# A state-space kernel in which 38 sums of GpSimd become accumulating transfers

## The reference, cut to what matters

```
def step(h, inputs):
    d_t, x_t, B_t, C_t = inputs
    dA = jnp.exp(d_t[..., None] * A)
    h = dA * h + (d_t * x_t)[..., None] * B_t[:, None, :]
    y = jnp.einsum('bds,bs->bd', h, C_t)
    return (h, y)
...
_, ys = jax.lax.scan(step, h0, xs)
y = ys.transpose(1, 0, 2) + xi * D
y = y * jax.nn.silu(z)
return x + y @ out_proj
```

## Time and profile before

| | |
|---|---|
| median of 3 runs | 586.09 us (582.63 to 587.27) |
| the profiled execution | 584.61 us, its span 582.8 us |
| mean granted TensorE clock | 0.935 |
| busy: PE, DVE, POOL, ACT | 81%, 79%, 69%, 64% of the span |

### The profile page before, as it was taken

One profiled execution on the slowest core, in us unless ns is written; L12 is line 12 of the kernel. 1 busy time (PEld: TensorE's weight loads), 2 busy tenths in 40 slices (PEclk: granted clock), 3 DMA queues, 4 the chain that ended last, 5 costly groups with the idle time before them and its releaser, 6 DMA issues.

```text
span 582.8 us, 7918 instructions
## 1 busy us (share of the span) xinstructions
PE 473.5 (81%) x2753; PEld 336.4 (58%) x2753; DVE 461.4 (79%) x531; ACT 374.3 (64%) x650; POOL 404.1 (69%) x253
## 2 busy tenths in 40 slices
PE   8968988778668899988678899795798758889992
PEld 6424655455547565745466466564686546678651
DVE  4779969988996678979987679789989989961512
ACT  3766667679764666788757567897747758821210
POOL 5049799859895599879883998888869979610001
PEclk9979999978998999869999999699999989999997
DMA  9331011111011011110210101101101292029004
GB/s 287 103 111 36 37 37 37 38 38 36 37 36 37 0 38 58 51 40 1 70 40 1 36 37 39 37 37 37 43 33 46 85 401 91 2 65 359 1 1 149
DMA packets 17919, 38.88 MB, mean 67 GB/s; under 512 B 1665, under 2 KB 10497, under 8 KB 17874
## 3 DMA queue, kind: packets, MB, share of 16 engines
q1 hardware_dynamic: 17874, 38.32, 18.5%
HBM read 36.08 MB, written 2.23 MB: 66 GB/s over the span
## 4 chain that ended last, share of the span: by engine, by line
PE 37%; DVE 24%; issue 15%; ACT 12%; POOL 9%; DMA 1%; DVEq 0%; SPq 0%; ACTq 0%; POOLq 0%
DVE scanmem L1742 13%; PE hT L824 8%; POOL scanmem L1393 6%; PE pp L616 5%; PE pp L553 4%; DVE yTd L1762 4%; PE pp L529 4%; ACT hc L1257 2%; PE yacc L587 2%; PE dA L789 2%; POOL yTd L1407 2%; DVE yTd L1667 1%; ACT dA L1247 1%; PE pp L688 1%; PE pp L579 1%
## 5 line engine op out<-in xcount | busy, mean ns | idle before, releaser
L1393 POOL TENSOR_TENSOR scanmem<-par,scanmem 128x1024 f32<-128x1024 f32 x128 | 300.0, 2360 | 56.6 <-ACT carry L1272 23.7
L1247 ACT ACTIVATE dA<-par,Aneg 128x512 f32<-128x512 f32 x256 | 172.7, 690 | 58.7 <-DVE scanmem L1742 57.1
L824 PE MATMUL hT<-con,scanmem 128*128 128x128 f32 x1024 | 155.5, 290 | 61.3 <-DVE yTd L1762 39.9
L824 PEld LDWEIGHTS hT<-con,scanmem 128*128 128x128 f32 x1024 | 120.4, 148 | 115.1 <-DVE yTd L1762 51.2
L1742 DVE TENSOR_TENSOR_SCAN scanmem<-dA,carry,scanmem 128x512 f32<-128x512 f32 x128 | 156.6, 1268 | 5.0 <-ACT dA L1247 4.7
L1742 DVE TENSOR_TENSOR_SCAN scanmem<-dA,scanmem 128x512 f32<-128x512 f32 x128 | 149.1, 1207 | 6.1 <-ACT dA L1247 5.8
L1257 ACT ACTIVATE hc<-hT,CTs 128x512 f32<-128x512 f32 x128 | 87.2, 681 | 67.5 <-PE hT L824 67.1
L587 PE MATMUL yacc<-con,hc 128*128 128x128 f32 x512 | 77.1, 293 | 6.2 <-ACT hc L1257 6.1
L1762 DVE SCALAR_TENSOR_TENSOR yTd<-hT,CTs,yTd 128x512 f32<-128x512 f32 x82 | 59.9, 731 | 16.6 <-POOL yTd L1407 11.2
L587 PEld LDWEIGHTS yacc<-con,hc 128*128 128x128 f32 x512 | 63.6, 151 | 10.1 <-ACT hc L1257 7.3
L529 PE MATMUL pp<-xnT,wi 128*128 128x512 f32 x120 | 60.9, 637 | 5.3 <-ACT xnT L1023 3.2
(11 more groups left out here) (198 smaller groups left out, 530.3 us busy)
## 6 DMA issues: line engine op xcount, KB each, us to landing
scanmem<-brow SPq DMA_DIRECT2D x32, 512.0 KB, 3.5
par<-in SPq DMA_DIRECT2D x1, 4096.0 KB, 17.6
scanmem<-in SPq DMA_DIRECT2D x1, 4096.0 KB, 14.4
xt<-in SPq DMA_DIRECT2D x4, 512.0 KB, 6.7
wi<-in SPq DMA_DIRECT2D x2, 1024.0 KB, 7.0
out<-par SPq DMA_DIRECT2D x4, 512.0 KB, 4.1
aw<-in SPq DMA_DIRECT2D x5, 256.0 KB, 6.6
xr<-in SPq DMA_DIRECT2D x1, 1024.0 KB, 10.0
```

Source lines behind the costliest of these rows:

```text
L824: last = nc.tensor.transpose(hT[:, i % 2, m * P:(m + 1) * P], hb[:, n % RING, m, i * P:(i + 1) * P], ident)
L1247: A(dA[:, m % 2, :], delta(c)[:, m, :], ACT.Exp, scale=Aneg[:, m * NS + s:m * NS + s + 1]).then_inc(da_ready, 1)
L1393: nc.gpsimd.tensor_tensor(hb[:, n % RING, ms, :], dx(c)[:, ms, :], Bb[:, row:row + 1, :].to_broadcast([P, 2, T]), ALU.mult).then_inc(bx_re ...
```

## The change

The addition on GpSimd becomes a transfer that GpSimd issues, which reads `for_pool(n)` and accumulates it into the same 128x512 tile of `yTd` (256 KB). Its semaphore rises by 16 when it has landed, so every wait on `pool_sum_done` counts in sixteens. Nobody may pass before the transfer is complete.

```
@@ job_Y, TensorE
                 if i == 3 and by_pool(n):
-                    pe.wait_ge(pool_sum_done, pool_sums(n))
+                    pe.wait_ge(pool_sum_done, 16 * (pool_sums(n)))
@@ pool_mul_step, ScalarE
                     if pool_sums(n) > 2:
-                        act.wait_ge(pool_sum_done, pool_sums(n) - 2)
+                        act.wait_ge(pool_sum_done, 16 * (pool_sums(n) - 2))
@@ add_step, GpSimd
                     if by_pool(n - 1):
-                        pool.wait_ge(pool_sum_done, pool_sums(n - 1))
+                        pool.wait_ge(pool_sum_done, 16 * (pool_sums(n - 1)))
...
                     dst = yTd[:, c % 2, 1, :]
-                    nc.gpsimd.tensor_tensor(dst, dst, for_pool(n), ALU.add).then_inc(pool_sum_done, 1)
+                    nc.gpsimd.dma_start(out=dst, in_=for_pool(n), accum_op=ALU.add).then_inc(pool_sum_done, 16)
@@ mac_step, VectorE
                     if i == 3 and by_pool(n - 1):
-                        dve.wait_ge(pool_sum_done, pool_sums(n - 1))
+                        dve.wait_ge(pool_sum_done, 16 * (pool_sums(n - 1)))
```

## The result

The changed kernel takes 612.38 us (median of 4 runs, 610.91 to 613.99) against 586.44 us before: a ratio of 1.0455, with an interval of 1.0416 to 1.0494. The prediction was 607, 592 to 640. The profiled executions are 612.23 and 584.61 us, with spans of 610.4 and 582.8: 27.6 us to explain. Ratios compare the fast runs as a whole and times are medians of all runs, so the two can differ by some tenths of a per cent.

The account below looks back on a forecast made before the run. No engine is full; engines wait for each other in a cycle, so when a sum lands counts. Later landings of 16.4 us plus 5 us of clock make 21 us on 584.6: 607 us, range 592 to 640.

Parts of the forecast that it names:

- six places: Engines stand waiting for the sums of steps 1, 17, 33 (7.9 us), 15 and 31 (5.5), 47 (1.4).
- the covered gaps: Other 15 sums of chunks 0 to 2, needed 2.0 to 8.5 us after their end; four shortest cost 1.6 us.
- the clock: Longer TensorE pauses at steps 1, 31, 33 and 47: four more drops to 1.2 GHz, 5 us in all.
- The price of a landing: Time from a 256 KB accumulating transfer's issue until it lands: 4.0 us, between ends of 2.0 and 6.6.
- The 3.5 of the B rows: Landing time of 512 KB B-row transfers in the trace before, 3.5 us, taken as nearest to the new transfer.
- the 0.5 for GpSimd's preparation: Estimated 0.5 us added to the landing because GpSimd prepares in its own stream what SP hands over.
- d: Time by which a sum lands later than GpSimd's 1.27 us addition: 4.0 - 1.27 = 2.73 us.
- Steps 3, 19 and 35: Short gaps of 0.3, 1.0 and 0.1 us; GpSimd and VectorE both move by about the same delay, nothing added.
- Step 62: Last sum of the loop's final chunk, needed by VectorE 2.94 us after its end: 0 us.
- the other direction, VectorE holding up GpSimd's transfer: VectorE in two-port modes keeps GpSimd from writing descriptors: about 12 us more, 619 us; chance 0.05 alone.
- Chunk 3: Its 14 sums: GpSimd waits for one before issuing the next, starts at least 3.7 us apart; counted at nothing.
- GpSimd's relief: Rival: GpSimd's freed 48.3 us of additions count as in the chain, 2% or 11 us faster, 575 us; chance 0.02.

Follow-up runs that it names:

- the two runs that split the sums: Changed kernel with the sums of steps 1, 15, 17, 31, 33, 47 added by GpSimd again: 595.19 us; with only these as transfers: 605.16 us.
- the products in the pause: Changed kernel plus 13 identity products on TensorE ahead of its waits for the transfers of steps 15, 31 and 47: 605.63 us (26 products: 609.58).

## Why the prediction was right

*Direction, size and place* held. The sum was 21 us, measured 26 on the medians and 27.6 on the profiled executions. The six places were named, and the two runs that split the sums confirm them. That the time came within 5 us is in part luck: the waits at the six places and the covered gaps were taken 6.4 us too large, the clock 6 too small, and the 7.2 of the two other places were not in the sum. With the landing that was measured, its own terms give 10 + 5 = 15 us, some 601 us and not 612.

*The price of a landing* was mis-sized: 4.0 for 3.2. The 3.5 of the B rows, taken as the base, was 0.3 too much. No run shows the 0.5 for GpSimd's preparation by itself: a plain copy that GpSimd issues lands in 2.3 us, between SyncE's 2.0 for 64 KB and 3.5 for 512 KB. So d is 1.9 instead of 2.73, and the waits at the six places cost 6.0 + 5.3 - 1.3 = 10 us instead of 14.8.

*The clock* was mis-sized the other way: 5 us for four drops. The six places fell back 21.0 us, of which 10 are waits; the other 11 I put down to matmuls at 1.2 GHz. I had counted only pauses that newly drop the clock, once each, and not that the clock falls further behind 15 and 17, where it was already low in part (behind 17 it is 0.58 from 217 to 224 us, 0.76 before from 202 to 209). That it is the clock is shown for 3.8 us at 31 and 47 by the products in the pause, and for a part that is not known at 15. At 1, 17 and 33 it is read from the trace alone; the delay at step 1 was between 2.1 and 4.8 us in executions that have the same transfer there.

*Steps 3, 19 and 35* were rightly counted at nothing, for the reason given: they opened once the sums ahead of them were added again.

*The covered gaps*, 1.6 us in the sum, cost next to nothing: at d = 1.9 only at steps 13 and 39 does VectorE start 0.1 us behind the landing, with no idle time. Step 62 cost nothing, as said, and ScalarE waited 0.2 us once.

*The held VectorE instruction* was the failed step. The prediction had only the other direction, VectorE holding up GpSimd's transfer, and gave it 0.05, because "VectorE's loop instructions read one operand from PSUM". I had looked at the instructions that each step repeats and not at those that run once inside the loop. Step 7 shows it, with 4.9 us, and the run that adds this one sum again gives the time back. Steps 57 to 59 show the same picture at line 1593, which takes 3.55 us for 2.14 before; no run changes that one alone.

*Chunk 3* was put at nothing, with GpSimd's waiting for its own sums "covered by its inputs' lead on the scans" and few transfers of SyncE in the loop. The loads for the last stages were not reckoned with: three transfers landed in 7.2 to 8.7 us, outside the 3.2 to 5.0, and GpSimd waited 1.70 us for one of them. That these loads are what made them late is read from the trace and not tested.

*GpSimd's relief* was rightly refused, but its busy time fell 12.5 us and not the 48 that was given as a sign, since an issue holds it 0.9 and the inputs behind it are longer. VectorE's scans wait for its inputs 0.3 us as before.

## What to carry to other kernels

Before work is handed to a transfer, list for each instance who waits for it and how much later it may come; the price of the longer latency is paid at the few places without slack, and a pause there costs TensorE's clock as well. If a result is waited for, first look whether it can be issued earlier in its engine's order: moving 38 sums ahead of one input gained 16 us with additions and 29 with transfers, while turning the additions into transfers cost 26 us in the one order and 13 in the other. And search a loop also for what runs once in it, small instructions and loads for later stages.

## What the runs showed of the hardware that was not expected

A VectorE instruction of 0.17 us, alone, took 3.17 us behind an issue of GpSimd and the 2.64 us input that followed. An accumulating transfer of 256 KB within SBUF landed in 3.2 us, a copy of the same size in 2.3, an accumulating one of 64 KB also in 2.3; it held GpSimd for 0.9 us. Beside loads that kept the DMA engines at a share of 0.86 to 1.08, three accumulating transfers of 256 KB took 7.2 to 8.7 us. Three us of idle products in each of three pauses gave back 6.8 us.
